# Graph network layers on one core: four-head attention with the edge tiles as weights

## What is computed

```python
# layer 0: maximum of h over the first 25 neighbours, joined to h, times W, relu
# layer 1: four heads of 64
Wh = (h @ W).reshape(B, N, 4, 64)
e = leaky_relu(e_src[:, :, None, :] + e_dst[:, None, :, :], 0.2)
e = where(adj > 0, e, -1e9)
x = x + elu(einsum('bijh,bjhf->bihf', softmax(e, axis=2), Wh))
# layer 2: mean over incoming edges
x = x + relu(h @ W_upd + einsum('bij,biu->bju', adj, h @ W_msg) / max(deg, 1) + bias)
# layer 3: the same attention with one head of 256 and no elu
x = x + einsum('bij,bjd->bid', softmax(e), h @ W.T)
```

## Time and profile before

| | |
|---|---|
| median of 3 runs | 6539.77 us (6536.77 to 6539.8) |
| the profiled execution | 6541.7 us |
| its span | 6539.8 us |
| PE busy | 5101.5 us, 78% |
| DVE busy | 4692.1 us, 72% |
| POOL busy | 3433.4 us, 53% |
| ACT busy | 2100.4 us, 32% |

### The profile page before, as it was taken

The page is one execution under the profiler, slowest core; times in us unless marked ns, Lnnn a source line. Parts: engine busy times, 40 slices in busy tenths (PEclk is TensorE's granted clock), DMA queues, the critical chain, the costliest instruction groups (busy, mean ns, idle before and its releaser), DMA issues.

```text
span 6539.8 us, 85786 instructions
## 1 busy us (share of the span) xinstructions
PE 5101.5 (78%) x23860; PEld 3069.3 (47%) x23860; DVE 4692.1 (72%) x9897; ACT 2100.4 (32%) x4103; POOL 3433.4 (53%) x3204
## 2 busy tenths in 40 slices
PE   2224987889768887789887897788977888778998
PEld 1113336643457335563366533564345733565367
DVE  6766876678767786778867787677866777665833
ACT  3223134331342314432243313523144222432131
POOL 5777337761577427774277724775167732771000
PEclk8555988889889998889988898898988999889999
DMA  5545128441574317652285414853166521841040
GB/s 185 171 149 162 48 80 256 145 134 38 149 225 140 99 38 224 187 157 65 62 254 151 148 38 120 236 152 106 33 193 202 156 63 50 251 138 45 1 129 14
DMA packets 660534, 848.88 MB, mean 130 GB/s; under 512 B 80356, under 2 KB 491752, under 8 KB 659944
## 3 DMA queue, kind: packets, MB, share of 16 engines
q0 software_dynamic: 153600, 419.64, 21.9%
q10 hardware_dynamic: 344064, 268.50, 14.0%
q1 hardware_dynamic: 162408, 155.53, 7.4%
HBM read 774.13 MB, written 69.21 MB: 129 GB/s over the span
## 4 chain that ended last, share of the span: by engine, by line
PE 49%; DVE 19%; DMA 13%; issue 8%; POOL 5%; ACT 3%; ACTq 2%; DVEq 1%; SPq 0%; POOLq 0%
PE acc L938 23%; PE acc L942 12%; POOL gath L595 5%; DMA hb<-in_adj 5%; PE acc L886 4%; DVE gath L1135 4%; DMA col_i<-in_adj 3%; DVE edge L1239 3%; PE psH L855 2%; DVE top L1030 2%; DVE cat L1143 2%; DMA gath<-htab,idx 2%; DVE key L1033 2%; PE psB L905 1%; PE acc L970 1%
## 5 line engine op out<-in xcount | busy, mean ns | idle before, releaser
L595 POOL DMA_INDIRECT gath<-htab,idx x3200 | 3433.2, 1073 | 2482.7 <-issue 2241.2
L1239 DVE SCALAR_TENSOR_TENSOR edge<-region,gg,adjT 128x1024 f32<-128x1024 f32 (+1 forms) x1536 | 1639.6, 1107 | 471.6 <-ACT region L729 233.6
L938 PE MATMUL acc<-edge,region 128*65 128x512 f32 x4096 | 1840.1, 602 | 57.5 <-DVE edge L1239 37.2
L942 PE MATMUL acc<-region,edge 128*128 128x257 f32 x4096 | 996.8, 401 | 145.3 <-DVE xr L1278 87.6
L938 PEld LDWEIGHTS acc<-edge,region 128*65 128x65 f32 x4096 | 554.8, 140 | 1150.0 <-issue 1023.6
L1135 DVE TENSOR_TENSOR gath<-gath 128x1536 f32<-128x1536 f32 (+2 forms) x672 | 784.1, 1180 | 232.1 <-DMA gath<-htab,idx 179.3
L942 PEld LDWEIGHTS acc<-region,edge 128*128 128x128 f32 x4096 | 804.4, 200 | 284.9 <-issue 100.5
L886 PE MATMUL acc<-w_s,edge 128*128 128x512 f32 (+2 forms) x1536 | 579.7, 522 | 0.2 <-DVE region L1180 0.2
L1030 DVE MAX8 top<-key 128x8 f32<-128x256 f32 (+1 forms) x1024 | 408.1, 399 | 79.7 <-DVE key L1033 36.4
L637 ACT ACTIVATE adjT_b<-psT 128x1024 bf16<-128x1024 bf16 x256 | 262.5, 1025 | 487.4 <-PE psT L824 473.1
L970 PE MATMUL acc<-region,col_b 128*128 128x257 bf16 x1024 | 295.0, 288 | 146.4 <-ACT col_b L784 87.1
(11 more groups left out here) (130 smaller groups left out, 5818.9 us busy)
## 6 DMA issues: line engine op xcount, KB each, us to landing
adj_i<-in_adj ACTq DMA_DIRECT2D x512, 256.0 KB
hb<-in_adj ACTq DMA_DIRECT2D x256, 256.0 KB
col_i<-in_adj ACTq DMA_DIRECT2D x256, 256.0 KB
gath<-htab,idx POOLq DMA_INDIRECT x3200
cat<-htab SPq DMA_DIRECT2D x128, 128.0 KB
x<-in_x SPq DMA_DIRECT2D x128, 128.0 KB
x1d<-x SPq DMA_DIRECT2D x128, 128.0 KB
xr<-x1d SPq DMA_DIRECT2D x32, 512.0 KB, 4.5
```

Source lines behind the costliest of these rows:

```text
L595: pool.indirect_dma_start(out=gath[:, par, s, :], out_offset=None, in_=htab, in_offset=bass.IndirectOffsetOnAxis(ap=idx[:, par, s:s + 1], ...
L938: ins = pe.matmul(acc[0:F + 1, 2 * h + half, :], V[1][:, J, (F + 1) * head:(F + 1) * (head + 1)], here[:, 512 * half:512 * half + 512], st ...
L942: ins = pe.matmul(acc[:, k, 0:C + 1], here[:, P * k:P * k + P], V[3][:, J, :], start=(J == 0), stop=(J == NT - 1), skip_group_check=True)
L1239: dve.scalar_tensor_tensor(ring[p][:, n % EDGES[p], :], wB_of[p][:, h, :], gg[:, J, head:head + 1], adjT[:, J, bass.ds(((b + (p - 1)) % 2) ...
```

## The change

attend1 now works as attend3 does. The eight 128 x 128 pieces of an edge tile are the weights, the 65 columns of V for one head move, and node tile t with head h lands in bank t // 2 at column 65 * (2 * (t % 2) + h). Nothing is turned: `yT`, `turn_back` and the evacuation on ACT are gone. `result` on DVE reads the bank itself, all four calls for a quarter standing at the head of the next one, and PE waits for them bank by bank (`y_ok`). `add` comes after the edges of J = 0, 2, 4 and 6.

Other edits: in attend3 all four rows of factors have places of their own (`wB_of[3]`), those of quarters 1 to 3 being made at J = 4, 8 and 12 of quarter 0; `x3_ok` is told bank by bank, and `attend_end` stands one J later. In the mean, the loads of columns go on from one quarter to the next throughout, the first two are asked for in prep2, PE waits for the last split only at m = 3, and `norm(3, b, 0)` moves from before prep3 into quarter 2. hT has other places in SBUF. PE's first matmuls of a prep wait for the banks, where before its first transposes did. `norm(2, b, 0)` moves to the head of quarter 3. Each pair of attend1 and of the mean stands in a loop of one turn.

```diff
-                 3: region[:, val_cols:val_cols + 512].rearrange("p (h i) -> p h i", h=1)}
+                 3: region[:, val_cols:val_cols + NQ * 512].rearrange("p (h i) -> p h i", h=NQ)}
...
-        x3_ok = count("x3_ok", 1)
-
-        yT_ok, back_ok, y_ok, e_ok = count("yT_ok", 4), count("back_ok"), count("y_ok", 1), count("e_ok")
+        x3_ok = count("x3_ok", BLK)
+
+        y_ok, e_ok = count("y_ok"), count("e_ok")
...
-                    return [lambda k=k, m=m: do.mean(b, q, k, m, odd) for k in range(BLK) for m in range(4)]
+                    steps = [lambda k=k, m=m: do.mean(b, q, k, m) for k in range(BLK) for m in range(4)]
+                    if q == 2:
+                        steps.insert(4, lambda: do.norm(3, b, 0))
+                    return steps
...
-                        steps.insert(1, lambda: do.attend_end(3, b, q - 1))
+                        steps.insert(2, lambda: do.attend_end(3, b, q - 1))
...
+                for k in reversed(range(BLK)):
+                    steps.insert(ADD_AT[k], lambda k=k: do.add(b, q - 1, k))
+                steps = [lambda k=k: do.result(b, q - 1, k) for k in range(BLK)] + steps
+                if q == NQ // 2 + 1:
+                    steps.insert(0, lambda: do.norm(2, b, 0))
                 if q == NQ - 1:
...
+                    steps += [lambda k=k: do.result(b, q, k) for k in range(BLK)]
+                    steps += [lambda k=k: do.add(b, q, k) for k in range(BLK)]
                 return steps
...
-                if phase == "mean":
-                    with eng.Fori(0, NQ // 2) as r:
-                        pair(phase, r, n, lambda i: (r * (n // 2) + (s + i) // 2, i % 2), None)
-                else:
-                    for r in range(NQ // 2):
+                for r in range(NQ // 2):
+                    with eng.Fori(0, 1) if phase in ("attend1", "mean") else nullcontext():
                         pair(phase, r, n, lambda i: ((s + n * r + i) // 2, (s + n * r + i) % 2), pre_done + n * r if early else None)
...
+                        if p == 2 and n == GROUPS - 2:
+                            for first in range(2):
+                                self.load_columns(b, 0, 0, first)
...
+                    if p == 3 and q == 0 and J in ROW_AT:
+                        self.attend_start(p, b, 1 + ROW_AT.index(J))
...
-                    elif not odd:
+                    elif q < NQ - 1:
                         self.load_columns(b, q + 1, 0, then % 4)
...
-                            for half in range(2):
-                                if ahead and half == 1:
+                            for t in range(2 * BLK):
+                                k, at = t // 2, (F + 1) * (2 * (t % 2) + h)
+                                if ahead and t == BLK:
                                     self.spread_row(p, b, q + 1, h, 1)
-                                if J == 0:
-                                    pe.wait_ge(yT_ok.sem, yT_ok.free(HEADS * Q + 2 * h + half, HEADS))
-                                ins = pe.matmul(acc[0:F + 1, 2 * h + half, :], V[1][:, J, (F + 1) * head:(F + 1) * (head + 1)],
-                                                here[:, 512 * half:512 * half + 512], start=(J == 0), stop=(J == NT - 1), skip_group_check=True)
+                                first = J == 0 and h == 0 and t % 2 == 0
+                                if first and q > 0:
+                                    pe.wait_ge(y_ok.sem, y_ok.ready(BLK * (Q - 1) + k))
+                                ins = pe.matmul(acc[:, k, at:at + F + 1], here[:, P * t:P * t + P], V[1][:, J, (F + 1) * head:(F + 1) * (head + 1)],
+                                                start=first, stop=(J == NT - 1), skip_group_check=True)
...
+                                if J == 0:
+                                    pe.wait_ge(x3_ok.sem, x3_ok.free(BLK * Q + k, BLK))
...
-                        if k == 0:
-                            pe.wait_ge(ev_ok[2].sem, ev_ok[2].ready(GROUPS * b + GROUPS - 1))
+                        if q == 0 and k == 0:
+                            pe.wait_ge(ev_ok[2].sem, ev_ok[2].ready(GROUPS * b + GROUPS - 2))
...
+                    if q == 0 and k == 0 and m == 3:
+                        pe.wait_ge(ev_ok[2].sem, ev_ok[2].ready(GROUPS * b + GROUPS - 1))
...
-                    dve.wait_ge(back_ok.sem, back_ok.ready(n))
-                    sums = psB[:, 0:HEADS * (F + 1)].rearrange("p (h f) -> p h f", h=HEADS)
+                    if k == 0:
+                        dve.wait_ge(mm_ok[1].sem, mm_ok[1].ready(2 * NT * (NQ * b + q) + 2 * NT - 1))
+                    sums = acc[:, k, 0:HEADS * (F + 1)].rearrange("p (h f) -> p h f", h=HEADS)
```

More of the change, by code:

```diff
@@ L28 @@
-from contextlib import ExitStack
+from contextlib import ExitStack, nullcontext
 import concourse.bass as bass
@@ L435, in ahead, with mean @@
             def ahead(self, T, part): pass
-            def mean(self, b, q, k, m, odd): pass
+            def mean(self, b, q, k, m): pass
             def end(self, b): pass
@@ L725, in row_weights @@
                     H, Q = wide(p), NQ * b + q
-                    if half == 0:
+                    row = h if p == 1 else q
+                    if p == 1 and half == 0:
                         act.wait_ge(edge_ok[p].sem, edge_ok[p].ready(NT * H * Q - H + h))
+                    if p == 3:
+                        act.wait_ge(edge_ok[p].sem, edge_ok[p].ready(NT * NQ * b - 1))
                     act.wait_ge(sB_ok[p].sem, sB_ok[p].ready(wide(p) * (H * Q + h) + half))
-                    act.activation(wB_of[p][:, h, 512 * half:512 * half + 512], psB[:, :], ACT.Exp, scale=1 - SLOPE).then_inc(wB_ok[p].sem, 1)
+                    act.activation(wB_of[p][:, row, 512 * half:512 * half + 512], psB[:, :], ACT.Exp, scale=1 - SLOPE).then_inc(wB_ok[p].sem, 1)
                 def attend_start(self, p, b, q):
@@ L775, in load_columns, with mean @@
                     act.dma_start(cols[m], adj_r[:, bass.ds(NT * b + 4 * m, 4), bass.ds((4 * q + k) * P, P)]).then_inc(c_ld[m], 16)
-                def mean(self, b, q, k, m, odd):
+                def mean(self, b, q, k, m):
                     J = 4 * (NQ * b + q) + k
-                    if k == 0 and m == 0 and not odd:
-                        for first in range(2):
-                            self.load_columns(b, q, 0, first)
                     act.wait_ge(c_ld[m], 16 * J + 16)
@@ L784, in mean @@
                     act.activation(cols_b[m], cols[m], ACT.Copy).then_inc(c_cast.sem, 1)
-                    if k == 0 and m == 0 and not odd:
+                    if q == 0 and k == 0 and m == 0:
                         act.wait_ge(ev_ok[2].sem, ev_ok[2].ready(GROUPS * b + GROUPS - 1))
```

89 lines of the change are left out of this document (27 added, 62 removed).

## The result

The changed kernel takes **7693.93 us** (median of 4 runs, 7683.58 to 7739.18) against 6538.27 for the kernel before on the same chip (4 runs, 6532.88 to 6539.8): ratio 1.178, 95% interval 1.174 to 1.1821. It is 17.8% slower; the forecast was 7664 us, 17% slower. The profiled execution took 7739.18 us (span 7737.3), the upper end of its runs.

The account below looks back on a forecast made before the run. PE was taken to bound the four-head attention, with DVE close behind. Seven batches of +157 - 25 us (924) and +200 for the last added 1124 to 6540, giving 7664 us, range 7350 to 8150.

Parts of the forecast that it names:

- Term 1: Four-head attention (attend1): each of 2048 records costs its 128-column weight load, 0.110 us at 2.4 GHz, 0.213 at 1.2.
- the rival of a load as cheap as a transpose's: Four-head attention: 0.061 us a record, the clock rises, DVE bounds the stage at 250 us; 6156 us total; chance 3%.
- loads and matmuls run one after the other: Rival in four-head attention: 161 ns a record at 2.4 GHz, 320 at 1.2; some 9200 or 7200 us; chance 5%.
- Term 2: Four-head attention: mostly at half clock, 512 records at 0.110 us and 1536 at 0.213, 383 us.
- my first rival: Four-head attention: the clock holds at 2.4 GHz, stage 272 us as before, total 6340 us; chance 11%.
- Term 3: Quarter boundaries in four-head attention: PE idles 4.5 us three times a batch, 13.5 us; four results and activations at the end, 5.
- The stage: Four-head attention as a whole: 430 us against 273, +157 us a batch; 468 in the last batch.
- Term 4: Blocks outside four-head attention, mainly the mean and one-head attention: shorter waits save 25 us a batch.
- PE's 9.06 in the middle of the mean: Mean stage: the hole at a loop turn shrinks to 2 us by asking for columns across it, -7 us a batch.
- the 10.32 for the norm: End of the mean: PE's wait for layer 3's norm goes, since it now runs in the third quarter, -8 us.
- 1 us each stays: One-head attention (attend3): three waits for DVE's xr, 11.4 us together, shrink to 1 us each, -8 us.
- The sum: Whole kernel: seven batches at 157 - 25 give 924 us, the last +200, so +1124 us to 7664.

Follow-up runs that it names:

- padded kernel: The changed kernel moving 128 columns instead of 65, 63 of them useless: 8261.88 us, ratio 1.0348 to the kernel before; on another chip 6632.95 us, ratio 1.0142.
- the first experiment: The changed kernel with attend1 put back as before and all other edits kept: 8002.86 us, ratio 1.0055 to the kernel before.

## Why the prediction was right, step by step

**Term 1, a record costs its load: right.** Forecast 0.110 us at 2.4 GHz and 0.213 at 1.2. Of 16210 steps from record to record of line 928, 10843 are of 0.213 or 0.214 and 5146 of 0.111 or 0.112. The padded kernel has 0.111 to 0.113 with 128 moving columns, the one with 33 has 0.213 at the low clock: over 33 to 128 columns the step doesn't depend on what moves. This excludes the rival of a load as cheap as a transpose's (0.061) too. The best row of before for it was the lone load of line 897, a matmul of 4 columns that hides nothing. That loads and matmuls run one after the other is excluded: at 2.4 GHz the load (107 ns) and 65 columns (54) would make 0.161. The Trainium skill ("TensorE: Matmul & The Clock Gate", Part 3, the mechanism) says that they overlap only where their row groups differ; these use the same 128 rows (the forecast's "which is this case" is a slip), and the trace disagrees: 0.112. The same section of the Trainium skill also lets a load go ahead into a background weight buffer, and with that the trace agrees.

**Term 2, the clock: the mechanism right, its size a little off.** The forecast had the stage start at 0.50, stay there until line 841 (855 of before) and run two thirds of the 768 records behind it at 2.4 GHz: 512 of 2048. The two thirds were a guess between none and all. The trace has 792 to 804 steps of 0.11 in each of the first six stages, which is all of the 768 and some at the ends of quarters; 408 in the seventh, where the second run of line 841 raised nothing; and 17 in the last, nearly none, as forecast. With 802 records at 0.112 and 1246 at 0.213 the sum for the fourth is 355 us where I had 383; line 928 measured 358.0. The clock forecast of 0.55 to 0.70 came out at 0.63 (seventh batch 0.56), the last batch at 0.50. Why the clock rose behind 13 runs of line 841 and not behind the fourteenth, the runs don't show. That an engine busy without a hole can be held at 1.2 GHz was the step on which all hung, and the three experiments on moving columns show it: 33, 65 and 128 of them behind the same loads give the last batch 464, 464 and 260 us. The Trainium skill (the same page, Part 1, what is happening), read literally, gives this stage 2.4 GHz and the whole kernel the 6340 us of my first rival; the row of the last batch, PE busy 447.92 of 463.6 at 0.50, disagrees with that reading.

**Term 3, the boundaries: right, too small.** Forecast 3 x 4.5 = 13.5 us and 5 for the tail; measured 6.60, 5.55 and 6.84 = 19.0, and 4.33. In the last batch, without slots, they are 3.7 each: the sum of four `result` and one edge was near, even a little high, for DVE left alone, and in the other batches DVE and ACT have a slot's work between them as well. Cost beyond the forecast: 5.5 us a batch.

**The stage** came out at 407.9 against 430: -25 on the records, +5.5 on the boundaries, and the rest in transposes and slots. The seventh came out at 440.5, 170 over before where I had 157 for all seven, and the last at 463.6 against 468.

**Term 4, the other blocks: wrong.** Forecast -25 us a batch; measured -11 us over all eight. Both holes did go, PE's 9.06 in the middle of the mean and the 10.32 for the norm; a wait of 3.82 for a column tile is new, near the start of the mean. But the time came back. In the fourth batch the mean gained 148.6 - 144.0 = 4.6 us, and prep3 lost it: 51.4 (between the mean and attend3 in the earlier trace rows) to 58.2 us. Waits of PE in the mean and prep3 of the fourth batch after (us, times, longest):

```profile
PE psH L835 <- issue: 21.6, 5, 8.0
PE acc L950 <- DVE region L1160: 6.3, 1, 6.3
PE acc L950 <- ACT col_b L770: 6.0, 7, 3.8
```

Line 835 turns a slot's `cat`; before, it waited 5.0 us there, once. The slot's chain is a gather on POOL, then DVE's halving of it (18.7 us of waits for the gather's DMA in that stretch, the longest 8.1), then `cat`; as I read it, PE arrives earlier and the slot's data doesn't, so PE waits for that instead. ("issue" stands where the profile shows nothing that ended the wait.) The waits over the whole span agree: those for the norm and for column tiles fell by 127 us, and those ahead of line 835 (849 in the kernel before) rose by 156. Before, then after:

```profile
PE psH L849 <- issue: 313.7, 37, 29.2
PE psB L865 <- ACT hb L682: 143.2, 17, 17.6
PE acc L970 <- ACT col_b L784: 87.1, 53, 9.1
PE psH L849 <- DVE cat L1143: 51.4, 3, 17.9
...
PE psH L835 <- issue: 378.0, 62, 29.3
PE psH L835 <- DVE cat L1123: 143.4, 8, 19.4
PE psB L851 <- ACT hb L673: 51.8, 9, 17.7
PE acc L950 <- ACT col_b L770: 51.1, 52, 4.3
```

In attend3 I had three waits for `xr` fall from 11.4 us to 3. They take 11.0:

```profile
PE acc L934 <- DVE xr L1259: 11.0, 3, 5.4
```

Releasing a bank at a time didn't shorten them; the stage gained 3 us, not 8. The failed step is "1 us each stays": I took a finer release for an earlier one; by these waits the first `xr` comes no earlier, which no run tested by itself. That the others are worth nothing is shown by two measurements (ratio 1.0055 on the first chip; on the third, all but attend1 of the padded kernel takes 6631.8 - 2246.4 = 4385 us, and of the kernel before 6527.8 - 2142.7 = 4385). That it is the slot's chain that takes the mean's gain is read from the waits alone; no run moved that chain by itself.

**The sum.** Forecast +1124 us: +1321 for attend1, -197 for the rest. The profiled execution has +1209 and -11. So two errors of 112 and 186 us worked against each other, and the median lies 45 us under the profiled execution besides. That 7664 lies within 30 us of 7694 is luck; by its terms the forecast was good to a tenth in attend1 and wrong outside it.

## What to carry to other kernels

Swapping weights and values to cut streaming trades moving columns for weight loads: where a matmul moves fewer columns than it loads (here 33 or 65 against 128, in f32), its price is the load, and a stage of such matmuls can sit at the half clock however busy the profile shows PE. So price such a change at both clock levels, from a lone load and from stretches at either level, and look for what dense work stands near and for the holes behind it: here the level came with the one and went with the other. A hole that you remove in a stage fed by an independent chain (here the slots) is worth only the slack until that chain's next result; look up when that arrives before you count the gain.

## What was not expected

- Padding makes the kernel faster: 63 useless columns on nearly all of 16384 records took the ratio to before from 1.178 to 1.0142, and leaving out 32 of 65 columns gave 1.2335 on the first chip, where the nearest measure of the changed kernel is 1.1818 on the second.
- The same 65-column records hold the level they find: 47 us at 1.00 behind line 841, 100 us at 0.50 behind a boundary. With 33 columns 1.00 lasted some 3 us.
- On two chips the kernel before took 7976 and 7961 us, on the others 6538: 22% more. In the first experiment, on the first of them, the old attend1 took 270 to 280 us (last batch 245.0), nearly as in the kernel before here, and the stages with slots and many DMAs were longer: a mean took 208.6 us with DMA 0.64 busy, in the changed kernel here 144.0 with 0.91. The padded kernel's ratios were 0.02 apart between two chips. What differs between them I can't say; the stages without DMA are the ones to compare.
